# First layer of a two-layer transformer kernel: the order of TensorE's work in an attention slot, with one score chunk made a slot ahead and projections moved in front of the turned blocks

## The chip, the cores and the metric

One core of a Trainium2 chip. The metric is the device time of one execution in microseconds (us). TensorE does the matmuls, ScalarE (ACT) the exponentials and half of the copies out of PSUM, VectorE (DVE) the row maxima and the other copies, GpSimd (POOL) some elementwise work, and SyncE (SP) issues the DMAs. Each engine runs its own list of instructions in the order in which the program gives them; semaphores hold an instruction back until another engine has got far enough.

## The reference, cut to what matters

Eight batches of 512 tokens of 128 features go through two layers. The change is in the attention of the first layer, which has 16 heads of 64:

```
q = einsum('qdh,bcd->bhcq', Q, x) * sq          # x is layer-normed
k = einsum('qdh,bcd->bhcq', K, x) * sq
v = einsum('vdh,bcd->bhcv', V, x) * sv
att = einsum('bhcq,bhCq->bhcC', q, k) / d_query  # causal mask
p = softmax(att)
y = einsum('bhcC,bhCv->bhcv', p, v)
z = einsum('dvh,bhcv->bcd', W, y) * ...
```

Beside it stands a mixture of experts (32 experts and a shared one), worked as 17 units of gate, up and down products. The second layer is not touched.

## The kernel before

The first layer goes batch by batch. A batch has eight rounds, one for each pair of heads (PAIRS = 8), and then 17 expert units. A round n needs, in this order of data:

- its queries and keys: project_qk on TensorE (three products each, since every operand is split in a high and a low part), round_q and round_k on ACT (the high part), rest_q and rest_k on DVE (the low part);
- the scores in three chunks: chunk 0 is the last tile of 128 rows against 512 columns, chunk 1 is tiles 2 and 0, chunk 2 is tile 1 (CHUNKS). Each chunk fills two PSUM banks, one for each head. Score products use 64 rows of the array for each head;
- row_maxima on DVE, then exps on ACT, which write probs;
- the turned blocks: 20 transposes of 128x128 in five steps (turn_step, numbers 0, 1, 4, 3, 2 in TensorE's order), each into one bank. DVE copies steps 0, 1, 3 and 2 to the tile pt (take_turned), ACT copies step 4 (take_tile1);
- weigh_pair, the products of the turned blocks with the values, into bank 6; ACT copies the result to yt (copy_y).

PSUM has eight banks, and all of this shares them, so much of the order comes from banks: a turned step can't be written before the one that held its bank is copied, and a chunk of scores not before the bank's last reader is done. Before the change the five turned steps use banks 4 and 5 in turn, chunks 0 and 2 use banks 0 and 1, and chunk 1 banks 2 and 3.

TensorE's order is written out in slot. Slot n (n not the first of a batch) turns round n-1 and scores round n: turned steps 0 and 1 of n-1, queries n+1, chunk 0 of n, turned step 4, keys n+1, turned steps 3 and 2, chunks 1 and 2 of n, weigh_pair of n-1. The first slot of a batch (first_head) ends the batch before: two last expert units and the output projection (project_out) stand between its chunks. The function units begins with the turned steps of the last round, between the halves of the first expert unit. Each first_layer function (one in the program of ACT, one in that of DVE) holds the matching order of its engine. On DVE, route spreads the router's work over the slots.

Semaphores that matter here: pt_ready counts DVE's copies of turned steps (four in a round), pt4_ready ACT's one, y_ready ACT's copies of weighed values, qk_lo_ready the low parts, exp_done and max_ready the chunks.

Of the kernel before, what the change touches and what calls it, by code (L numbers as in the profile page):

```python
# [43 lines left out]
NCH = len(CHUNKS)  # L44
SCORE_BANK = [0, 2, 0]
SCORE_COL = {3: 0, 2: 0, 0: 384, 1: 0}
# [35 lines left out]
def build(nc, a, out_dram):  # L82
    with ExitStack() as ctx:
# [145 lines left out]
        def own_bank(n, s):  # L229


            return n >= ROUNDS0 and s == 2 and (n - ROUNDS0) % (2 * G) in range(2, 2 * G, 2)

        def turn_bank(n, s):
            return bank[6] if own_bank(n, s) else bank[TURN_BANK[s]]

# [3 lines left out]
        def rows_bank(b):  # L240

            return bank[6] if b < B - 1 else bank[7]

        UNIT_BANKS = [bank[0:2], bank[2:4]]

        def qk_banks(n):

            if n < ROUNDS0 and n % PAIRS < 2:
                return (bank[4], bank[5]) if n % PAIRS == 0 else (bank[6], bank[5])
            return bank[6], bank[7]  # L250
# [124 lines left out]

        def max_count(n, c):
            return n * NCH + ([1, 2, 3] if first_round(n) else [1, 3, 2])[c]

        def score_bank(n, c):

            return [6, 0, 6][c] if n >= ROUNDS0 and first_round(n) else SCORE_BANK[c]

# [323 lines left out]
        def _(act):  # L706
# [41 lines left out]
            def exps(rnd, c):  # L748
# [7 lines left out]
                last.then_inc(exp_done, 1)  # L756

            def take_values(b, fills):
# [51 lines left out]
            def copy_combt(b):  # L810
                act.wait_ge(combt_done, b + 1)
                act.activation(combt, bank[7][:, 0:P], ACT.Copy).then_inc(combt_ready, 1)

            def first_layer(b):
# [4 lines left out]
                for p in range(PAIRS):  # L819
                    n = b * PAIRS + p  # L820
                    if p == 0:
                        exps(n, 0)
                    if p < PAIRS - 1:
                        round_q(n + 1, SCALE0)
                    if p:
                        take_tile1(n - 1)
                        exps(n, 0)
                    if p < PAIRS - 1:
                        round_k(n + 1)
                    else:  # L830
                        copy_combt(b)
                    if p == 0:
                        exps(n, 1)
                    exps(n, 2)
                    if p == 0 and b:
                        copy_acc(b - 1)
# [5 lines left out]
                    if p:  # L842
                        copy_y(n - 1)
                        exps(n, 1)
# [5 lines left out]
                take_tile1(b * PAIRS + PAIRS - 1)  # L850
                for u in range(UNITS):
# [143 lines left out]
        def _(dve):  # L995
# [184 lines left out]
            def first_layer(b):  # L1180
                for p in range(PAIRS):
                    n = b * PAIRS + p
                    if p == 0:
                        row_maxima(n, 0)
                        row_maxima(n, 1)
                        rest_q(n + 1, SCALE0)
                        rest_k(n + 1)
                        row_maxima(n, 2)
                    else:
# [3 lines left out]
                        if p < PAIRS - 1:  # L1193
                            rest_q(n + 1, SCALE0)
                        elif b:
                            add_rows(b - 1)
                        take_turned(n - 1, [3, 2])
                        row_maxima(n, 2)
                        if p < PAIRS - 1:
                            rest_k(n + 1)  # L1200
                        row_maxima(n, 1)
                    route(b, p)
                n = b * PAIRS + PAIRS - 1
                take_turned(n, range(0, 2))
                invert_sums(n)
                for u in range(UNITS):
# [174 lines left out]
        def _(pe):  # L1381
# [78 lines left out]
            def turn_step(rnd, s):  # L1460
# [15 lines left out]
                if s == 3:  # L1476
                    pe.wait_ge(pt_ready, rnd * (TURNS - 1) + 2)
                blocks = [(s % 2, 3, j) for j in range(4)] if s < 2 else [(s % 2, 2, j) for j in range(3)] + [(s % 2, 0, 0)]
                if s == 4:
# [40 lines left out]
            def project_unit(b, u):  # L1520
                n = b * UNITS + u
                if u >= 2:
                    pe.wait_ge(su_done, n - 1)
                else:
                    pe.wait_ge(exp_done, exp_count((b + 1) * PAIRS - 1, 2 - u))
                half_unit(b, u, 0)
# [56 lines left out]
            def turn_weights(b):  # L1583

                pe.wait_ge(comb_ready, b + 1)
                nc.tensor.transpose(bank[7][:, 0:P], rexp[:, :, :].rearrange("p t e -> p (t e)"), ident[:, :]).then_inc(combt_done, 1)

            def score0(n, c):
                score_chunk(n, c, n % 2, ROWS0)

            def first_chunks(b):
                n = b * PAIRS
                pe.wait_ge(qk_lo_ready, n * 2 + 2)
                if b:
                    pe.wait_ge(su_done, b * UNITS)
                score0(n, 0)

            def slot(n, head):
# [6 lines left out]
                if p == 1:  # L1605
                    pe.wait_ge(qk_lo_ready, n * 2 + 2)
                turn_step(n - 1, 0)
                turn_step(n - 1, 1)
                if p < PAIRS - 1:
                    pe.wait_ge(y_ready, n - 1) if p > 1 else pe.wait_ge(qk_lo_ready, n * 2 + 1)  # L1610
                    project_qk(n + 1, [0])
                pe.wait_ge(qk_lo_ready, n * 2 + 2)
                pe.wait_ge(exp_done, exp_count(n - 1, 2))
                score0(n, 0)
                turn_step(n - 1, 4)
                if p == 1:
                    pe.wait_ge(acc_copied, b) if b else pe.wait_ge(logits_taken, 1)
                if p < PAIRS - 1:
                    project_qk(n + 1, [1])
                else:  # L1620
                    turn_weights(b)
                    pe.wait_ge(y_ready, n - 1)
                    if b:
                        turn_acc(b - 1)
                turn_step(n - 1, 3)
                turn_step(n - 1, 2)
                score_rest(n, n % 2, ROWS0)
                if p < PAIRS - 1:
                    pe.wait_ge(qk_lo_ready, (n + 1) * 2 + 1)
                elif b:  # L1630
                    pe.wait_ge(x1_ready, b)
                weigh_pair(n - 1)

            def first_head(b):

                if b:
                    project_out(b - 1, 0)
# [3 lines left out]
                    unit_down(b - 1, UNITS - 1)  # L1641
                first_chunks(b)
                score0(b * PAIRS, 1)
                if b:
                    project_out(b - 1, 2)
                pe.wait_ge(v_taken, (b + 1) * FILLS)
                project_qk(b * PAIRS + 1, range(2))
                pe.wait_ge(exp_done, exp_count(b * PAIRS, 0))
                score0(b * PAIRS, 2)
                if b:  # L1650
                    project_out(b - 1, 3).then_inc(acc_done, 1)

            def units(b):
                n = (b + 1) * PAIRS - 1
                turn_step(n, 0)
                turn_step(n, 1)
                pe.wait_ge(exp_done, exp_count(n, 2))
                half_unit(b, 0, 0)
                turn_step(n, 4)
                half_unit(b, 0, 1).then_inc(gu_done, 1)  # L1660
                turn_step(n, 3)
                turn_step(n, 2)
                project_unit(b, 1)
# [38 lines left out]
            for b in range(B):  # L1702
                if b == 1:
                    pe.wait_ge(act_setup, 1)
                for p in range(PAIRS):
                    slot(b * PAIRS + p, lambda: first_head(b))
                if b == 0:
# [285 lines left out]
```

## Time and profile before

| | |
|---|---|
| median of 3 runs | 1213.09 us (1210.03 to 1213.88) |
| span of the profiled execution | 1209.2 us (first to last instruction; what lies around it is not in the profile) |
| TensorE busy | 1189.8 us, 98% |
| DVE busy | 990.7 us, 82% |
| ACT busy | 819.7 us, 68% |
| GpSimd busy | 409.9 us, 34% |
| granted TensorE clock | 1.000 |

A busy TensorE in this table is one that has an instruction under way by a modelled end; gaps of a few tenths between products can be inside it. Times in the trace are counted from the start of the span. Each batch of the first layer takes about 121 us, and its attention part, from the first score product to the transpose that follows the last weigh_pair (line 1495), 75.7 us.

### The profile page before, as it was taken

The numbers are of one execution on the slowest core, as the hardware profiler recorded it, in microseconds if no ns is written. First come the engines' busy times: TensorE is split into PE (matmuls) and PEld (weight loads), VectorE is DVE, ScalarE is ACT, GpSimd is POOL, SyncE is SP. The second block draws the span as 40 slices with busy tenths as digits, with TensorE's granted clock in tenths as the row PEclk, the third lists the DMA queues.
The fourth block names the chain that finished last, engine by engine and source line by source line (L and its number), as shares of the span: only waits on it lengthen the run. The fifth ranks groups of instructions, "written<-read, shape, count | busy, mean of one in ns | idle before, by whom it ended". The sixth has DMA issues, their size and how long they took to land.

```text
span 1209.2 us, 23949 instructions
## 1 busy us (share of the span) xinstructions
PE 1189.8 (98%) x8908; PEld 887.1 (73%) x8908; DVE 990.7 (82%) x1918; ACT 819.7 (68%) x2174; POOL 409.9 (34%) x364
## 2 busy tenths in 40 slices
PE   8999999999999999999999999999999999999998
PEld 6777677767776777677767776777677767767766
DVE  6888588968886889688968896888788878988886
ACT  6785577567756775677567756775677768767875
POOL 2216420640064006400640064006400658535820
PEclk9999999999999999999999999999999999999999
DMA  7004300410041004200420042004200420000000
GB/s 258 1 30 134 97 1 21 132 61 2 20 134 62 1 19 134 62 1 19 135 62 1 20 134 62 1 17 136 62 1 16 138 62 2 7 12 19 1 11 27
DMA packets 44292, 63.93 MB, mean 53 GB/s; under 512 B 8144, under 2 KB 18384, under 8 KB 43920
## 3 DMA queue, kind: packets, MB, share of 16 engines
q1 hardware_dynamic: 44176, 62.39, 16.6%
q8 instruction: 72, 1.18, 0.4%
q14 instruction: 44, 0.36, 0.1%
HBM read 59.48 MB, written 2.88 MB: 52 GB/s over the span
## 4 chain that ended last, share of the span: by engine, by line
PE 82%; DVE 10%; ACT 4%; issue 2%; DMA 1%; SPq 1%; POOL 0%; DVEq 0%; ACTq 0%; POOLq 0%
PE psum L1435 14%; PE psum L1483 14%; PE psum L1505 12%; PE psum L64 9%; PE psum L66 9%; PE psum L65 9%; PE psum L1542 5%; DVE mneg L1123 2%; ACT probs L754 2%; PE psum L1444 2%; PE psum L1718 1%; DVE sg L1173 1%; PE psum L1509 1%; PE psum L1781 1%; DVE sg L1163 1%
## 5 line engine op out<-in xcount | busy, mean ns | idle before, releaser
L754 ACT ACTIVATE probs<-psum,mneg 128x512 f32<-128x512 f32 (+3 forms) x640 | 329.7, 529 | 127.1 <-DVE mneg L1123 122.5
L1123 DVE TENSOR_REDUCE mneg<-psum 128x2 f32<-128x1024 f32 (+2 forms) x320 | 253.6, 820 | 99.9 <-PE psum L1444 99.5
L1114 DVE COPY pt<-psum 128x512 f32<-128x512 f32 x320 | 205.2, 682 | 29.7 <-PE psum L1483 27.9
L1483 PE MATMUL psum<-ident,probs 128*128 128x128 f32 x1600 | 223.3, 278 | 6.1 <-DVE pt L1114 2.1
L1483 PEld LDWEIGHTS psum<-ident,probs 128*128 128x128 f32 x1600 | 176.5, 140 | 37.9 <-issue 19.5
L561 POOL TENSOR_TENSOR qk_lo<-sg,qk_hi 128x512 fp32r<-128x512 f32 x64 | 92.7, 1455 | 162.0 <-ACT qk_hi L798 162.0
L525 POOL TENSOR_TENSOR rstd<-var,mhalf 128x4 f32<-128x4 f32 x7 | 7.1, 1012 | 399.8 <-DVE var L1009 399.8
L1505 PE MATMUL psum<-pt,v_all 128*64 128x384 f32 (+5 forms) x1088 | 142.6, 412 | 0.0
L754 ACT ACTIVATION_READ_ACCUMULATOR probs<-psum,mneg 128x1 f32 x640 | 131.8, 206 | 0.0
L1435 PE MATMUL psum<-qk_hi 64*128 64x512 f32 (+7 forms) x640 | 121.6, 375 | 2.2 <-ACT probs L754 1.9
L1505 PEld LDWEIGHTS psum<-pt,v_all 128*64 128x64 f32 (+1 forms) x1088 | 69.5, 135 | 66.2 <-issue 50.7
L64 PE MATMUL psum<-xt_hi,gu_hi 128*128 128x512 f32 x272 | 110.7, 407 | 0.0
L66 PE MATMUL psum<-xt_hi,gu_lo 128*128 128x512 f32 x272 | 107.7, 396 | 0.0
L65 PE MATMUL psum<-xt_lo,gu_hi 128*128 128x512 f32 x272 | 107.4, 395 | 0.0
L557 POOL TENSOR_TENSOR yt<-yt,rrow 128x512 f32<-128x512 f32 x64 | 99.2, 1556 | 21.4 <-DMA rrow<-sums 21.3
L1435 PE MATMUL psum<-qk_lo,qk_hi 64*128 64x512 f32 (+7 forms) x640 | 103.5, 319 | 0.0
L1435 PE MATMUL psum<-qk_hi,qk_lo 64*128 64x512 f32 (+7 forms) x640 | 103.3, 318 | 0.0
L1173 DVE TENSOR_TENSOR sg<-sg,crow 128x512 f32<-128x512 f32 x88 | 96.4, 1096 | 6.0 <-DMA crow<-weights 3.1
L808 ACT ACTIVATE sg<-psum 128x512 f32<-128x512 f32 x96 | 57.1, 595 | 54.1 <-PE psum L66 53.9
L1435 PEld LDWEIGHTS psum<-qk_hi 64*128 64x128 f32 (+1 forms) x640 | 60.1, 184 | 42.9 <-issue 38.4
L1163 DVE TENSOR_TENSOR sg<-sg,psum 128x512 f32<-128x512 f32 x96 | 65.3, 680 | 20.1 <-ACT sg L808 20.1
L798 ACT ACTIVATE qk_hi<-sg 128x512 fp32r<-128x512 f32 x96 | 60.3, 628 | 31.3 <-DVE sg L1173 31.3
(275 smaller groups left out, 2422.4 us busy)
## 6 DMA issues: line engine op xcount, KB each, us to landing
crow<-weights SPq DMA_DIRECT2D x256, 128.0 KB, 3.0
rrow<-sums SPq DMA_DIRECT2D x128, 128.0 KB, 3.0
gu_raw<-in_gu SPq DMA_DIRECT2D x1, 2176.0 KB, 11.5
x_all<-in_x SPq DMA_DIRECT2D x8, 256.0 KB, 6.4
out_rows<-x_all SPq DMA_DIRECT2D x7, 256.0 KB, 2.3
down_raw<-in_down SPq DMA_DIRECT2D x1, 1088.0 KB, 13.7
wqkv_raw<-in_wqkv SPq DMA_DIRECT2D x1, 896.0 KB, 6.8
wqkv_raw<-in_wqkv SPq DMA_DIRECT2D x1, 512.0 KB, 5.0
```

What stands on the lines that cost most here:

```text
L64: nc.tensor.matmul(out, lh, rh, start=start, stop=False, **kw)
L65: nc.tensor.matmul(out, lh, rl, start=False, stop=False, **kw)
L66: return nc.tensor.matmul(out, ll, rh, start=False, stop=stop, **kw)
L557: pool.tensor_tensor(yt[:, p, :], yt[:, p, :], rrow[:, n % RROWS, :], ALU.mult).then_inc(y_divided, 1)
L561: pool.tensor_tensor(hm_lo[u % 3], sg[u % 3], hm_hi[u % 3].bitcast(F32), ALU.subtract).then_inc(pool_lo_ready, 1)
L754: last = act.activation(probs[:, h * HALF + PROB[t]:h * HALF + PROB[t] + w], bank[score_bank(rnd, c) + h][:, o:o + w], ACT.Exp, bias=mneg[ ...
L1114: dve.tensor_copy(turned_rows(rnd)[:, s % 2, :, 3 - s // 2, :], turn_bank(rnd, s).rearrange("p (j q) -> p j q", q=P)).then_inc(pt_ready, 1)
L1123: last = dve.tensor_reduce(mneg_h[:, :, t], psum[:, b:b + 2, o:o + P * (t + 1)], AX, ALU.max, negate=True)
L1173: dve.tensor_tensor(sg[u % 3], sg[u % 3], crow[:, m % CROWS, :], ALU.mult).then_inc(hm_ready, 1)
L1435: mm(bank[score_bank(rnd, c) + h][:, o:o + w], ql[r, 0, qs_], kl[r, 1, ks], start=i == 0 and n == 0, stop=False, **K)
L1483: last = nc.tensor.transpose(turn_bank(rnd, s)[:, i * P:(i + 1) * P], probs[:, v:v + P], ident[:, :])
L1505: last = mm(Y[c:c + m, first * P:T], v(k), rows_t[:, k, first:TILES, :].rearrange("p t q -> p (t q)"), start=(k == 0), stop=(k == TILES - ...
```

## The change

Three things are moved, and banks follow.

1. Slot n now does round n as a whole, but for its chunk 0: chunks 1 and 2 of n, chunk 0 of n+1 (score_group), then weigh_pair of n-1, queries and keys of n+2, and last all five turned steps of n. ACT makes the exponentials of chunk 0 of n+1 at the end of slot n (next_exps), after it has rounded the queries and keys of n+2.
2. Chunk 2's scores move to banks 4 and 5, and the five turned steps get a bank each: 2, 3, 7, 5, 4 (TURN_BANK0, for steps 0 to 4). Queries go to bank 7, keys to bank 6, except for the first two pairs of a batch. Steps are guarded by other waits than before (turn_step0).
3. The first slot of a batch projects round 1 directly behind its chunk 0 and rounds it on ACT before the exponentials of chunk 1; the projection of round 2 now waits in that slot for the copy of the batch before's output sum (acc_copied).

No operation is added or taken away. The core of the diff:

```diff
-SCORE_BANK = [0, 2, 0]
+SCORE_BANK = [0, 2, 4]
+        TURN_BANK0 = [2, 3, 7, 5, 4]
...
 # ACT, first_layer
                     if p == 0:
                         exps(n, 0)
+                        round_q(n + 1, SCALE0)
+                        round_k(n + 1)
+                    exps(n, 1)
+                    if p:
+                        copy_y(n - 1)
+                        exps(n, 2)
+                    else:
+                        exps(n, 2)
+                        if b:
+                            copy_acc(b - 1)
+                    if p < PAIRS - 2:
+                        round_q(n + 2, SCALE0)
+                        round_k(n + 2)
+                    if p == PAIRS - 2:
+                        copy_combt(b)
                     if p < PAIRS - 1:
-                        round_q(n + 1, SCALE0)
-                    if p:
-                        take_tile1(n - 1)
-                        exps(n, 0)
...
+                        next_exps(n + 1, 0)
+                        next_exps(n + 1, 1)
+                    take_tile1(n)
...
 # DVE, first_layer
-                        take_turned(n - 1, range(0, 2))
-                        row_maxima(n, 0)
-                        invert_sums(n - 1)
...
+                    row_maxima(n, 1)
+                    row_maxima(n, 2)
+                    if p < PAIRS - 1:
+                        row_maxima(n + 1, 0)
                     route(b, p)
+                    if p < PAIRS - 2:
+                        rest_q(n + 2, SCALE0)
+                    take_turned(n, [0])
+                    if p < PAIRS - 2:
+                        rest_k(n + 2)
+                    elif p == PAIRS - 1 and b:
+                        add_rows(b - 1)
+                    take_turned(n, [1])
+                    invert_sums(n)
+                    if p < PAIRS - 1:
+                        take_turned(n, [3, 2])
...
 # TensorE
+            def turn_step0(n, s):
+
+                b, p = n // PAIRS, n % PAIRS
+                pe.wait_ge(exp_done, exp_count(n, [1, 1, 2, 2, 2][s]))
+                if s == 2 and p < PAIRS - 2:
+                    pe.wait_ge(qk_lo_ready, (n + 2) * 2 + 1)
+                if s == 2 and p == PAIRS - 2:
+                    pe.wait_ge(combt_ready, b + 1)
+                turn_blocks(n, s)
+
+            def score_group(n):
+
+                b, p = n // PAIRS, n % PAIRS
+                if p:
+                    pe.wait_ge(pt_ready, (n - 1) * (TURNS - 1) + 2)
+                score0(n, 1)
+                if p:
+                    pe.wait_ge(pt4_ready, n)
+                    pe.wait_ge(pt_ready, (n - 1) * (TURNS - 1) + 3)
+                if p < PAIRS - 1:
+                    pe.wait_ge(qk_lo_ready, (n + 1) * 2 + 2)
+                score0(n, 2)
+                if p < PAIRS - 1:
+                    pe.wait_ge(exp_done, exp_count(n, 0))
+                    score0(n + 1, 0)
+
+            def slot(n):
...
                 if p == 0:
-                    head()
-                    return
...
+                    first_head(b)
+                score_group(n)
+                if p:
+                    weigh_pair(n - 1)
+                elif b:
+                    project_out(b - 1, 3).then_inc(acc_done, 1)
+                if p < PAIRS - 2:
+                    if p:
+                        project_qk(n + 2, [0])
+                        pe.wait_ge(y_ready, n)
+                        project_qk(n + 2, [1])
+                    else:
+                        pe.wait_ge(acc_copied, b) if b else pe.wait_ge(logits_taken, 1)
+                        project_qk(n + 2, range(2))
+                elif p == PAIRS - 2:
+                    turn_weights(b)
+                elif b:
+                    pe.wait_ge(y_ready, n)
+                    turn_acc(b - 1)
+                turn_step0(n, 0)
+                turn_step0(n, 1)
                 if p < PAIRS - 1:
...
+                    turn_step0(n, 4)
+                    turn_step0(n, 3)
+                    turn_step0(n, 2)
```

## Rows read from the trace of the kernel before

**Rows 1.** The page: span, parts 1 and 2.
```profile
span 1209.2 us, 23949 instructions
...
PE 1189.8 (98%) x8908; PEld 887.1 (73%) x8908; DVE 990.7 (82%) x1918; ACT 819.7 (68%) x2174; POOL 409.9 (34%) x364
...
PEclk9999999999999999999999999999999999999999
```

**Rows 2.** Waits of the whole span: engine, line, releaser: us in total, times, longest.
```profile
PE psum L1483 <- DVE pt L1114: 2.1, 5, 0.6
```

**Rows 3.** Windows: busy by engine (instructions), clock, DMA share, GB/s.
```profile
382.74:458.41 75.67, 75.67 (x676) 54.97 (x675) 61.42 (x122) 53.85 (x163) 2.02 (x2) 1.00 0.04 13
...
407.92:416.68 8.76, 8.76 (x84) 6.45 (x82) 7.30 (x17) 6.46 (x20) 0.00 (x0) 1.00 0.01 3
...
450.95:458.41 7.46, 7.46 (x54) 5.50 (x52) 5.07 (x9) 5.90 (x14) 2.02 (x2) 1.00 0.35 105
17.85:93.40 75.55, 72.91 (x664) 53.13 (x663) 62.84 (x121) 60.28 (x173) 18.18 (x14) 1.00 0.16 42
```

**Rows 4.** Timeline of TensorE in one slot: start, us, engine, line.
```profile
407.92 1.09 PE L1483 MATMUL psum<-ident,probs 128*128 128x128 f32 x8
...
409.63 0.18 PEld L1435 LDWEIGHTS psum<-qk_hi 64*128 64x128 f32 x2 [0.36 <-issue]
409.64 0.50 PE L1435 MATMUL psum<-qk_hi 64*128 64x512 f32 x2
...
410.62 0.66 PE L1483 MATMUL psum<-ident,probs 128*128 128x128 f32 x4
...
412.77 0.45 PE L1435 MATMUL psum<-qk_hi 64*128 64x384 f32 x2
...
414.37 2.16 PE L1505 MATMUL psum<-pt,v_all 128*64 128x384 f32 x16
```

**Rows 5.** Timeline of ACT in the same slot and the next one's start.
```profile
408.53 0.58 ACT L754 ACTIVATE probs<-psum,mneg 128x384 f32<-128x384 f32 x1
...
410.33 0.62 ACT L767 ACTIVATE qk_hi<-psum 128x512 fp32r<-128x512 f32 x1
...
411.99 0.69 ACT L754 ACTIVATE probs<-psum,mneg 128x512 f32<-128x512 f32 x1
...
415.10 0.47 ACT L754 ACTIVATE probs<-psum,mneg 128x256 f32<-128x256 f32 x1 [1.18 <-DVE mneg L1123]
...
415.93 0.20 ACT L754 ACTIVATION_READ_ACCUMULATOR probs<-psum,mneg 128x1 f32 x1
...
416.80 0.60 ACT L788 ACTIVATE yt<-psum 128x512 f32<-128x512 f32 x1 [0.67 <-PE psum L1509]
417.29 0.57 ACT L754 ACTIVATE probs<-psum,mneg 128x384 f32<-128x384 f32 x1
```

**Rows 6.** Timeline of DVE in the same slot.
```profile
410.73 1.23 DVE L1123 TENSOR_REDUCE mneg<-psum 128x2 f32<-128x1024 f32 x1 [0.76 <-PE psum L1444]
...
411.98 0.64 DVE L1103 SCALAR_TENSOR_TENSOR qk_lo<-psum,qk_hi 128x512 fp32r<-128x512 f32 x1
412.54 1.28 DVE L1114 COPY pt<-psum 128x512 f32<-128x512 f32 x2
...
414.99 0.68 DVE L1108 TENSOR_TENSOR qk_lo<-psum,qk_hi 128x512 fp32r<-128x512 f32 x1
...
415.58 1.28 DVE L1123 TENSOR_REDUCE mneg<-psum 128x2 f32<-128x768 f32 x2
```

**Rows 7.** Timeline of the first slot of the fourth batch.
```profile
387.44 0.60 ACT L767 ACTIVATE qk_hi<-psum 128x512 fp32r<-128x512 f32 x1 [0.91 <-PE psum L66]
...
388.06 0.69 DVE L1103 SCALAR_TENSOR_TENSOR qk_lo<-psum,qk_hi 128x512 fp32r<-128x512 f32 x1 [1.82 <-ACT qk_hi L767]
...
388.64 1.98 PE L1542 MATMUL psum<-yt,w_out 128*128 128x512 f32 x4
```

**Rows 8.** Timeline of ACT in the first batch: a weight split at a slot's end.
```profile
25.17 1.33 ACT L730 ACTIVATE gu_hi<-gu_raw 128x1280 fp32r<-128x1280 f32 x1
```

More of the change, by code:

```diff
@@ L232, in own_bank @@
             return n >= ROUNDS0 and s == 2 and (n - ROUNDS0) % (2 * G) in range(2, 2 * G, 2)
+        TURN_BANK0 = [2, 3, 7, 5, 4]
+        TURN_BANK0_FIRST = [2, 3, 7, 5, 4]
         def turn_bank(n, s):
+            if n < ROUNDS0:
+                return bank[(TURN_BANK0 if n % PAIRS else TURN_BANK0_FIRST)[s]]
             return bank[6] if own_bank(n, s) else bank[TURN_BANK[s]]
@@ L242, in rows_bank @@
             return bank[6] if b < B - 1 else bank[7]
+        WEIGHTS_BANK = bank[7]
         UNIT_BANKS = [bank[0:2], bank[2:4]]
         def qk_banks(n):
-            if n < ROUNDS0 and n % PAIRS < 2:
-                return (bank[4], bank[5]) if n % PAIRS == 0 else (bank[6], bank[5])
+            if n < ROUNDS0:
+                return (bank[4], bank[5]) if n % PAIRS == 0 else (bank[6], bank[5]) if n % PAIRS == 1 else (bank[7], bank[6])
             return bank[6], bank[7]
@@ L376, in max_count @@
         def max_count(n, c):
+            if n < ROUNDS0:
+                return n * NCH + c + 1
             return n * NCH + ([1, 2, 3] if first_round(n) else [1, 3, 2])[c]
         def score_bank(n, c):
-            return [6, 0, 6][c] if n >= ROUNDS0 and first_round(n) else SCORE_BANK[c]
+            if n < ROUNDS0:
+                return SCORE_BANK[c]
+            return [6, 0, 6][c] if first_round(n) else SCORE_BANK1[c]
         exp_count = max_count
@@ L756, in exps, with next_exps @@
                 last.then_inc(exp_done, 1)
+            def next_exps(rnd, h):
+                act.wait_ge(max_ready, max_count(rnd, 0))
+                act.wait_ge(turned, turn_count(rnd - 1, h))
+                t = CHUNKS[0][0]
+                o, s = h * HALF + PROB[t], slice(h * TILES + t, h * TILES + t + 1)
+                last = act.activation(probs[:, o:o + T], bank[score_bank(rnd, 0) + h], ACT.Exp, bias=mneg[:, s], accum_out=rsum[:, rnd % 2, s])
+                if h:
+                    last.then_inc(exp_done, 1)
             def take_values(b, fills):
@@ L811, in copy_combt @@
                 act.wait_ge(combt_done, b + 1)
-                act.activation(combt, bank[7][:, 0:P], ACT.Copy).then_inc(combt_ready, 1)
+                act.activation(combt, WEIGHTS_BANK[:, 0:P], ACT.Copy).then_inc(combt_ready, 1)
             def first_layer(b):
@@ L1585, in turn_weights @@
                 pe.wait_ge(comb_ready, b + 1)
-                nc.tensor.transpose(bank[7][:, 0:P], rexp[:, :, :].rearrange("p t e -> p (t e)"), ident[:, :]).then_inc(combt_done, 1)
+                nc.tensor.transpose(WEIGHTS_BANK[:, 0:P], rexp[:, :, :].rearrange("p t e -> p (t e)"), ident[:, :]).then_inc(combt_done, 1)
             def score0(n, c):
                 score_chunk(n, c, n % 2, ROWS0)
[L1591 to L1598, printed above, removed]
+            def turn_step0(n, s):
[21 more added lines that the diff above has]
+            def slot(n):
                 p = n % PAIRS
@@ L1602, in slot @@
                 if p == 0:
-                    head()
-                    return
[L1605 to L1608, printed above, removed]
-                if p < PAIRS - 1:
[L1610 to L1632, printed above, removed]
+                    first_head(b)
[19 more added lines that the diff above has]
+                turn_step0(n, 1)
+                if p < PAIRS - 1:
+                    turn_step0(n, 4)
+                    turn_step0(n, 3)
+                    turn_step0(n, 2)
             def first_head(b):
+                n = b * PAIRS
                 if b:
@@ L1641, in first_head @@
                     unit_down(b - 1, UNITS - 1)
-                first_chunks(b)
-                score0(b * PAIRS, 1)
+                pe.wait_ge(qk_lo_ready, n * 2 + 2)
+                if b:
+                    pe.wait_ge(su_done, b * UNITS)
+                score0(n, 0)
+                pe.wait_ge(v_taken, (b + 1) * FILLS)
+                project_qk(n + 1, range(2))
                 if b:
                     project_out(b - 1, 2)
[L1646 to L1651, printed above, removed]
             def units(b):
                 n = (b + 1) * PAIRS - 1
-                turn_step(n, 0)
-                turn_step(n, 1)
-                pe.wait_ge(exp_done, exp_count(n, 2))
                 half_unit(b, 0, 0)
-                turn_step(n, 4)
+                turn_step0(n, 4)
                 half_unit(b, 0, 1).then_inc(gu_done, 1)
-                turn_step(n, 3)
-                turn_step(n, 2)
+                turn_step0(n, 3)
+                turn_step0(n, 2)
+                pe.wait_ge(pt_ready, n * (TURNS - 1) + 2)
+                if b:
+                    pe.wait_ge(x1_ready, b)
                 project_unit(b, 1)
@@ L1705, in _ @@
                 for p in range(PAIRS):
-                    slot(b * PAIRS + p, lambda: first_head(b))
+                    slot(b * PAIRS + p)
                 if b == 0:
```

32 lines of the change are left out of this document (3 added, 29 removed).

## The prediction, made before the changed kernel was run

> **What bounds the kernel now.** I read the page first: TensorE is busy 98% of the span at full clock, the others have room [rows 1]. Busy ends are modelled, so I asked the waits whether it really never stands: in the whole span its longest entry of waiting for a copy of turned blocks is 2.1 us in 5 waits [rows 2]. Then the windows. The attention part of a batch takes 75.67 us without idle time on TensorE (75.6 to 75.7 in every batch but the first, which has 75.55 with 2.6 idle); inside it a plain slot takes 8.76 us, five times in a batch, while DVE works 7.30 to 7.8 and ACT 6.46 of it [rows 3]. So time is won only by making TensorE's own list shorter, and lost wherever the new order makes it stand. The rest of the work (31.87 of 75.67) lies in the first slot, the last two and the head of the units.
>
> **What the change takes away.** No operation goes. What goes is switching between score products (64 rows) and 128-row work: before a slot enters the scores twice, now once. The gap in front of such an entry is 0.36 in which weights waited for nothing shown, and chunk 0 with its masks takes 409.64 to 410.62 = 0.98, of which three product pairs at the 0.24 that follow one another and the masks' 0.08 explain 0.8 [rows 4]. One visit fewer is thus worth between 0 (masks now stand between score products, and the change from weighing to projecting is new and not in the trace) and 0.34; I take 0.17. TensorE alone would need 8.6 us for a slot. The Trainium skill (TensorE: Matmul & The Clock Gate, Step-by-step: what each phase is for) says that weight loads are pulled ahead of running matmuls where row groups don't conflict or a background buffer is free; read as always, that would leave no gap and so no gain, slots of 8.76. The 0.36 shows that a gap is there.
>
> **What the change makes wait: the plain slot (p = 1 to 5).** Before, five pieces lay between one round's steps, and everyone was served while TensorE did something else. Now all scores stand together, all turned steps stand together, and chunk 1 of slot n+1 may start only when DVE has copied steps 0 and 1 of n (banks 2 and 3). On DVE those copies stand behind rest_q(n+2), on ACT round_q(n+2) stands behind the exponentials of chunk 2, and those behind copy_y(n-1), which waits for this slot's weigh_pair. That is a ring. From the first product of chunk 1:
>
> - chunks 1 and 2 with their masks, 412.77 to 414.37: 1.60. Chunk 0 of n+1 inside the scores: 0.98 less the 0.10 of entering, 0.88. First weighing product to the start of copy_y, 414.37 to 416.80: 2.43. Together 4.91 [rows 4, 5]. ACT is free by then: the maxima of chunk 1 start some 1.2 in and take 1.28, the exponentials 408.53 to 410.33 = 1.80, so 4.33 [rows 5, 6].
> - ACT: copy_y to the next start 0.49; chunk 2's two exponentials 415.10 to about 416.03, 0.93; round_q 0.62 to its end [rows 5]; handing over 0.02 to 0.03 [rows 7]. 6.98 so far.
> - DVE: rest_q 0.56 to the next start; copy of step 0 0.60; rest_k 0.59; copy of step 1 0.68 to its end [rows 6]; 0.05 to TensorE. **9.46.**
>
> Can a step come later than its place in the ring? Step 0 is turned in time: keys are projected from 5.56 (y_ready), and keys with four transposes take less than the 1.72 of eight transposes and three products (407.92 to 409.64), 7.3 against the 7.54 at which DVE comes [rows 4]. round_k ends at 7.4, before 8.14. DVE's route (1.2 at most in a slot) lies in the 2.5 us for which it now waits in front of rest_q: nothing. ACT's chunk 0 (1.34, 411.99 to 413.33) and take_tile1 run from 7.5 to 9.2 and chunk 2 of the next slot wants them at 10.4: nothing [rows 5]. DVE ends steps 3 and 2 at 10.7, when the next maxima become due: nothing, but no room left. So TensorE, done at 8.6, stands some 0.85 in front of chunk 1, and a slot takes 9.46 for 8.76: +0.70, +3.5 for five.
>
> **The first slot (b > 0).** From chunk 0: maxima end at 2.33, exponentials at 3.70, round_q and round_k at 4.80, rest_k at 5.6. Chunk 1 stands behind the projections (1.4) and project_out (1.98 [rows 7]), starts at 4.5 and is scored at 5.75; maxima till 7.03, exponentials of chunks 1 and 2 (1.80 + 0.93) till 9.79, copy_acc till 10.39. TensorE has been done with project_out since 9.1 and stands: the projection of round 2 wants that bank. It starts at 10.44; round_q can start 0.97 later and takes 0.62, then the four DVE steps 2.43: chunk 1 of slot 1 at 14.5.
>
> **The last slots.** Slot 6 has no projections, so step 4 comes up at about 5.7, and chunk 2's exponentials end at 4.91 + 0.49 + 1.03 = 6.43; 12 transposes at 0.11 and the entry: 7.95. Slot 7 has no chunk 0: weighed at 4.03, ACT busy until 4.33, copy_y until 4.93, and turn_acc waits for it though TensorE was free at 3.9. Then 0.44 for turn_acc and the 7.46 that steps 0 and 1, the units' head and weigh_pair take unchanged [rows 3]: 12.9.
>
> **Sum.** 14.5 + 5 x 9.46 + 7.95 + 12.9 = 82.65 for 75.67: +7.0 a batch. In the first batch no project_out and no copy_acc: slot 0 12.7, the last 11.9, in all 79.9 for 75.55, +4.3; ACT's weight splits (1.33 [rows 8]) now follow take_tile1 and end at 10.6, before the next exponentials are due at 12. 7 x 7.0 + 4.3 = 53. Units and second layer keep their lists: 0. The span goes from 1209.2 to 1262; the median lies 3.9 above the span, so 1213.1 + 53 = **1266 us**.
>
> **The rivals.**
> - *The ring is hidden, the kernel gets faster.* TensorE then pays only its own list, 0.17 to 0.34 less in each of about 7 slots and 8 batches: 1194 to 1203. It needs a ring under 8.6. Even if weighed values came for free, ACT's other path (4.33 + 0.49 in place of 4.91 + 0.49) gives 8.88. So two copies or an order of waits would have to be other than I read them: 5%.
> - *The ring closes near the old slot, no change.* Decides at 8.7: three quarters of a us must be missing, partly by ACT or DVE being quicker when TensorE stands. With the first slot's wait still there: 1209 to 1220. 6%.
> - *DVE is the bound.* It has no room between step 2's copy and the next maxima. The ring would be DVE's: all its work at full durations, with every start after the end before. Then rest_q, copy and rest_k cost 0.64 + 0.68 + 0.68, not 1.75, slots take 9.7 and, as steps 3 and 2 come late as well, up to 10: 10 to 22 us more, 1276 to 1288. Against it: two copies took 1.28, not 2 x 0.68 [rows 6]. 9%. The Trainium skill (VectorE: DVE Perf Modes, The DRAIN you can't avoid) states just this, that the next op does not start until the pipe is empty; these rows disagree for ops that wait for nothing.
> - *Partly hidden.* First and last slots wait as worked out but plain slots take 9.0 to 9.2 (copies earlier than I place them): 1245 to 1256. 10%.
> - The forecast, 9.3 to 9.6 a plain slot and within 0.7 of my sum for the others: 1254 to 1278. 70%.
>
> **Range and chances.** 0.3% is about what a measurement of this kernel can tell from no change. 1247 to 1283 holds the forecast, most of the partly hidden case and half of DVE's: 8 in 10. Faster 0.05, within 0.3% 0.04, slower 0.91 (the no-change case reaches beyond 0.3% by a third).
>
> **What the trace after would show.** Plain slots of 9.46 from one first product of line 1435's 384-column form to the next; in front of each, TensorE idle for about 0.85 and released by DVE's copy (line of take_turned); ACT idle in front of copy_y by about 0.5; DVE idle for 1.5 to 2.5 in front of rest_q, released by round_q; in first slots about 1.3 released by copy_acc; in slots 7 about 1.0 released by copy_y. TensorE's busy share falls from 98% to about 94%, its clock stays. I am wrong if TensorE's idle time in front of chunk 1 is small, or if it is released by something else than the copy of step 1.

## The result, and the profile after

The changed kernel takes 1267.97 us (median of 4 runs, 1267.71 to 1269.03) for 1212.49 us of the kernel before (4 runs): 1.046 times as long, 95% interval 1.0443 to 1.0474. The forecast was 1266 with a range of 1247 to 1283. So the time grew by 55.5 us; the spans of the two profiled executions differ by 56.7, since the profiled one of the kernel before was about 1.5 us shorter than its median.

The page of the changed kernel: span, busy time, TensorE's busy tenths and clock in 40 slices, and the chain that ended last.

```profile
span 1265.9 us, 23805 instructions
...
PE 1190.5 (94%) x8908; PEld 894.5 (71%) x8908; DVE 978.4 (77%) x1918; ACT 810.0 (64%) x2174; POOL 406.3 (32%) x364
...
PE   8999999999999999999998999899989999999998
...
PEclk9999999999999999999999999999999999999999
...
PE 59%; DVE 20%; ACT 15%; issue 3%; DMA 1%; SPq 1%; POOL 0%; DVEq 0%; ACTq 0%; POOLq 0%
```

TensorE's matmuls (8908) and its busy time (1190.5 for 1189.8 [rows 1]) are the same; the span has grown by 56.7. So the time is idle time of TensorE, and the chain that ended last now runs through DVE and ACT for a third of the span; in the kernel before they had a seventh of it:

```profile
PE 82%; DVE 10%; ACT 4%; issue 2%; DMA 1%; SPq 1%; POOL 0%; DVEq 0%; ACTq 0%; POOLq 0%
```

The waits of TensorE in the whole span (line of the waiting work, releaser, us in total, times, longest) say where:

```profile
PE psum L1456 <- DVE pt L1137: 35.9, 48, 0.8
PE psum L65 <- ACT rrow L824: 7.8, 7, 1.1
PE psum L1571 <- ACT yt L810: 7.4, 7, 1.1
PE psum L1508 <- ACT probs L766: 5.5, 12, 0.7
PE psum L1456 <- DVE qk_lo L1131: 3.2, 8, 1.9
```

The first line is new: 48 times, in front of chunk 1 in slots 1 to 6 of each of the eight batches, the score products of line 1456 wait for DVE's copy of turned blocks, 35.9 us in all (before slot 1 the wait is 0.3, before the others 0.8). The second is the projection of round 2 waiting for copy_acc, the third turn_acc waiting for copy_y. The fourth is for the most part turned step 4 of slot 6 waiting for chunk 2's exponentials (0.5 in slot 6 of the fourth batch), the fifth the first slot's wait for rest_k, 1.9 in the first batch and 0.2 in the others. Together about 60 us.

Windows of the fourth batch, as in [rows 3]: the attention part, its first slot, a plain slot, slot 6; then the attention part of the first batch and three us of it. The columns are as in those rows; the number behind the five engines is the granted clock.

```profile
402.76:485.66 82.90, 75.58 (x676) 55.61 (x676) 60.82 (x122) 52.40 (x163) 2.02 (x2) 1.00 0.03 12
402.76:417.17 14.41, 12.79 (x87) 8.47 (x87) 7.99 (x13) 8.79 (x26) 0.00 (x0) 1.00 0.01 2
426.72:436.26 9.54, 8.70 (x83) 6.56 (x84) 7.21 (x18) 6.25 (x20) 0.00 (x0) 1.00 0.01 2
464.80:472.72 7.92, 7.44 (x78) 5.63 (x78) 6.73 (x15) 4.96 (x19) 0.00 (x0) 1.00 0.04 11
18.95:99.30 80.35, 72.93 (x664) 54.77 (x664) 60.26 (x122) 59.89 (x174) 17.88 (x14) 0.98 0.13 35
25.00:28.00 3.00, 3.00 (x22) 2.11 (x21) 2.12 (x4) 2.22 (x10) 0.00 (x0) 0.50 0.21 53
```

The part takes 82.90 for 75.67, +7.2; a plain slot 9.54 for 8.76, of which TensorE is busy 8.70. (Four of the five plain slots of a batch take 9.53 to 9.55, the fifth 9.46.) And the ring itself, one plain slot in the timeline:

```profile
426.72 0.45 PE L1456 MATMUL psum<-qk_hi 64*128 64x384 f32 x2 [0.84 <-DVE pt L1137]
...
427.73 0.37 PE L1456 MATMUL psum<-qk_hi 64*128 64x256 f32 x2
...
429.19 2.16 PE L1530 MATMUL psum<-pt,v_all 128*64 128x384 f32 x16
...
431.62 0.60 ACT L810 ACTIVATE yt<-psum 128x512 f32<-128x512 f32 x1 [0.39 <-PE psum L1534]
...
432.11 0.47 ACT L766 ACTIVATE probs<-psum,mneg 128x256 f32<-128x256 f32 x1
...
433.01 0.61 ACT L789 ACTIVATE qk_hi<-psum 128x512 fp32r<-128x512 f32 x1
...
433.07 2.35 PE L1508 MATMUL psum<-ident,probs 128*128 128x128 f32 x20
...
433.72 0.69 DVE L1126 SCALAR_TENSOR_TENSOR qk_lo<-psum,qk_hi 128x512 fp32r<-128x512 f32 x1 [2.22 <-ACT qk_hi L789]
434.33 0.68 DVE L1137 COPY pt<-psum 128x512 f32<-128x512 f32 x1
...
434.93 0.68 DVE L1131 TENSOR_TENSOR qk_lo<-psum,qk_hi 128x512 fp32r<-128x512 f32 x1
...
435.52 0.68 DVE L1137 COPY pt<-psum 128x512 f32<-128x512 f32 x1
...
436.26 0.45 PE L1456 MATMUL psum<-qk_hi 64*128 64x384 f32 x2 [0.84 <-DVE pt L1137]
```

Read it as a relay. Chunk 1 starts at 426.72; weigh_pair at 429.19; copy_y, which waited for it, at 431.62 (4.90 in); then on ACT chunk 2's exponentials and round_q (433.01); DVE had waited 2.22 for that one; then rest_q, step 0, rest_k, step 1, whose end at 436.20 lets chunk 1 of the next slot go, 9.54 after the first. TensorE stood for 0.84.

### The profile page after: what moved, and what is told of

Its sections match the earlier page's. It is cut to its first block, busy times and chain, and to the rows that moved or that the text cites. A ratio compares the mean times of both kernels' runs of the same rounds, so it can differ in the third digit from the quotient of the medians.

```text
span 1265.9 us, 23805 instructions
## 1 busy us (share of the span) xinstructions
PE 1190.5 (94%) x8908; PEld 894.5 (71%) x8908; DVE 978.4 (77%) x1918; ACT 810.0 (64%) x2174; POOL 406.3 (32%) x364
## 4 chain that ended last, share of the span: by engine, by line
PE 59%; DVE 20%; ACT 15%; issue 3%; DMA 1%; SPq 1%; POOL 0%; DVEq 0%; ACTq 0%; POOLq 0%
PE psum L1456 12%; PE psum L1530 10%; ACT probs L766 9%; PE psum L65 7%; PE psum L67 7%; PE psum L66 7%; DVE pt L1137 5%; DVE mneg L1146 4%; DVE qk_lo L1126 3%; PE psum L1508 3%; DVE qk_lo L1131 3%; ACT yt L810 3%; ACT qk_hi L789 2%; PE psum L1565 2%; PE psum L1465 2%
## 5 line engine op out<-in xcount | busy, mean ns | idle before, releaser
L766 ACT ACTIVATE probs<-psum,mneg 128x256 f32<-128x256 f32 (+3 forms) x528 | 254.3, 494 | 217.6 <-DVE mneg L1146 216.6
L1146 DVE TENSOR_REDUCE mneg<-psum 128x2 f32<-128x1024 f32 (+2 forms) x320 | 244.6, 819 | 45.9 <-PE psum L1465 43.9
L1508 PE MATMUL psum<-ident,probs 128*128 128x128 f32 x1600 | 199.8, 274 | 8.2 <-ACT probs L766 5.5
L1456 PE MATMUL psum<-qk_hi 64*128 64x512 f32 (+7 forms) x640 | 121.7, 376 | 40.9 <-DVE pt L1137 35.9
L1126 DVE SCALAR_TENSOR_TENSOR qk_lo<-psum,qk_hi 128x512 fp32r<-128x512 f32 x72 | 49.5, 688 | 119.2 <-ACT qk_hi L789 119.1
L1456 PEld LDWEIGHTS psum<-qk_hi 64*128 64x128 f32 (+1 forms) x640 | 60.6, 185 | 70.3 <-DVE pt L1137 47.3
L766 ACT ACTIVATION_READ_ACCUMULATOR probs<-psum,mneg 128x1 f32 x528 | 108.2, 205 | 0.0
```

The source lines that it names most:

```text
L766: last = act.activation(probs[:, h * HALF + PROB[t]:h * HALF + PROB[t] + w], bank[score_bank(rnd, c) + h][:, o:o + w], ACT.Exp, bias=mneg[ ...
L1146: last = dve.tensor_reduce(mneg_h[:, :, t], psum[:, b:b + 2, o:o + P * (t + 1)], AX, ALU.max, negate=True)
L1456: mm(bank[score_bank(rnd, c) + h][:, o:o + w], ql[r, 0, qs_], kl[r, 1, ks], start=i == 0 and n == 0, stop=False, **K)
L1508: last = nc.tensor.transpose(turn_bank(rnd, s)[:, i * P:(i + 1) * P], probs[:, v:v + P], ident[:, :])
```

## Experiments

Each kernel is the changed one with a short edit. Ratios are to the kernel before the change, from runs on the same chip.

**Is it the place in DVE's order, or DVE's amount of work?** Two edits: one moves work and adds none, the other adds work and moves none. The first moves the copy of step 1 ahead of rest_k:

```diff
-                    take_turned(n, [0])
+                    take_turned(n, [0, 1])
                     if p < PAIRS - 2:
                         rest_k(n + 2)
...
-                    take_turned(n, [1])
                     invert_sums(n)
```

> The changed kernel, but on DVE the copy of turned step 1 stands in front of rest_k, directly behind the copy of step 0. Same work, same amount. Theory (ring): rest_k, 0.60 to the next start, leaves the ring and nothing takes its place, since TensorE's own list is 8.70: plain slots go from 9.54 to 8.94, the first slot gains 0.2. About 3.2 us a batch, 25 in all: 1243. Rival (DVE's total work is the bound): the order on DVE changes nothing, 1268. Rival (the ring closes over chunk 2, which wants rest_k): plain slots stay within 0.1 of 9.54, 1264 to 1268.

Measured: 1255.5 us, ratio 1.036 (1.0343 to 1.0374); a plain slot 9.27, not 8.94. Moving work that stays the same in amount gains 12 us, so the order matters, but that is only half of the 25 that the ring gave. What was late next is in the timeline: chunk 2's first product (256 columns) comes 1.32 after chunk 1's, where in the changed kernel it was 1.01 (427.73 after 426.72).

```profile
430.14 0.44 PE L1455 MATMUL psum<-qk_hi 64*128 64x384 f32 x2 [0.24 <-DVE pt L1137]
...
430.72 1.24 DVE L1137 COPY pt<-psum 128x512 f32<-128x512 f32 x2
...
431.46 0.39 PE L1455 MATMUL psum<-qk_hi 64*128 64x256 f32 x2
```

The copies of steps 3 and 2 start at 430.72; the first of them ends at about 431.4, and chunk 2, which wants the bank of step 3, starts at 431.46. That copy had slipped behind rest_k; rest_k itself, ahead of it on DVE, can't have been the last thing awaited. Slot 6 became longer for the same reason, 8.24 for 7.92, while the first slot gained 0.4 (14.00 for 14.41).

The second edit adds work to DVE and moves nothing, one more reduction of 1.2 us a slot:

```diff
                     if p < PAIRS - 1:
+                        if p:
+                            bk = score_bank(n + 1, 0)
+                            dve.wait_ge(scored, max_count(n + 1, 0))
+                            dve.tensor_reduce(table_two, psum[:, bk:bk + 2, :], AX, ALU.max, negate=True)
                         row_maxima(n + 1, 0)
```

> The changed kernel with one more row maximum over two banks (1024 columns, 1.2 us) on DVE in each slot but the first and the last of a batch, in front of the maxima of chunk 0 of the next round; its result is used by nobody. It falls into the 2.2 us for which DVE waits in front of rest_q. Theory (ring): in most slots nothing, since 2.97 + 1.28 + 0.6 + 1.2 + 1.2 + route ends before round_q at 6.97; up to 0.3 where route is long: 1268 to 1275. Rival (DVE's total work is the bound): 1.2 us in each of 48 slots, 1326.

Measured: 1265.8 us, ratio 1.045 (1.0432 to 1.0467), the same as the changed kernel's 1.046 (1.0443 to 1.0474). The window of a plain slot is 9.54 with DVE at work for 8.55 of it:

```profile
435.07:444.61 9.54, 8.69 (x84) 6.55 (x84) 8.55 (x22) 6.24 (x20) 0.00 (x0) 1.00 0.01 3
```

DVE's total is not the bound: its work may grow by more than 1 us a slot for nothing, if it lands in the wait in front of rest_q.

**Both gates of DVE's order taken away.** Step 3 is copied before rest_k too, and TensorE waits for the low part of the keys where it needs them:

```diff
-                if p < PAIRS - 1:
+                if p == 0:
                     pe.wait_ge(qk_lo_ready, (n + 1) * 2 + 2)
                 score0(n, 2)
                 if p < PAIRS - 1:
+                    pe.wait_ge(qk_lo_ready, (n + 1) * 2 + 2)
...
 # DVE
-                    take_turned(n, [0])
+                    take_turned(n, [0, 1])
...
+                    take_turned(n, [3])
+                    invert_sums(n)
                     if p < PAIRS - 2:
                         rest_k(n + 2)
...
-                        take_turned(n, [3, 2])
+                        take_turned(n, [2])
```

> As the run with step 1 in front of rest_k, and besides DVE copies step 3 before rest_k too, and TensorE waits for the low part of the keys only behind chunk 2, where chunk 0 of the next round needs it. In the earlier run a plain slot took 9.26 and not 8.94, because chunk 2 waited 0.3 for the copy of step 3 (bank 5), which had slipped behind rest_k. Theory (ring, with that second gate taken away): plain slots 8.95, 0.3 x 5 x 8 = 12 us less than 1255: about 1243. Rival (the missing 0.3 is something else, as scores slowed by a neighbouring bank): slots stay at 9.26, 1255.

Measured: 1238.7 us, ratio 1.021 (1.0197 to 1.0228); a plain slot is 8.93, as the ring says. The 0.3 that was missing was step 3's bank. The total came out 4 us lower than I expected. I had counted 0.3 in plain slots alone; three of the five gained 0.33, and slot 6 came back from 8.24 to 7.91. That makes 1.8 a batch and 14.2 in all, and the two spans differ by 14.5 (1253.2 and 1238.7). The first slot stayed at 14.00. The medians, from different series, differ by 16.9, and the 2.4 between the two figures stay open.

```profile
425.18:434.11 8.93, 8.69 (x82) 6.54 (x83) 7.32 (x20) 6.16 (x21) 0.00 (x0) 1.00 0.01 2
```

**Is the wait for the weighed values part of the ring?** ACT does copy_y behind chunk 2's exponentials:

```diff
                     if p:
-                        copy_y(n - 1)
                         exps(n, 2)
+                        copy_y(n - 1)
```

> The changed kernel, but on ACT copy_y(n-1) stands behind the exponentials of chunk 2, not in front of them. Theory (the ring: weigh_pair, copy_y, exponentials of chunk 2, round_q, rest_q, copies of steps 0 and 1, chunk 1 of the next slot): the wait for weigh_pair leaves the ring, ACT's own list takes its place: 4.38 + 0.90 + 0.49, then the 3.25 from round_q on, so a plain slot goes from 9.54 to about 9.0. Slot 6 gains about 0.65 (step 4 waits less), slot 7 loses about 0.9 (turn_acc waits for a later copy_y). About 2.6 us a batch, 21 in all: 1247, still slower than before the change. Rival (DVE's work as a whole is the bound, or TensorE's own list): plain slots stay at 9.5, and with slot 7 later the time is the same or up to 7 us more: 1268 to 1275.

Measured: 1267.1 us, ratio 1.046 (1.0443 to 1.0479). My 1247 was wrong, and the rival's 1268 to 1275 comes close, but not for its reason: a plain slot went from 9.54 to 9.34, so the wait is in the ring. A batch without a fall of the clock gained 0.7 and not 2.6: plain slots gave 0.9, slot 6 the 0.7 that I expected (7.22 for 7.92), and the last slot took 0.9 back. Two things ate the rest. In the plain slot:

```profile
431.75 0.62 ACT L810 ACTIVATE yt<-psum 128x512 f32<-128x512 f32 x1
...
432.42 0.50 PE L65 MATMUL psum<-xt_hi,wqkv_hi 128*128 128x512 f32 x1 [0.21 <-ACT yt L810]
...
433.86 0.69 DVE L1137 COPY pt<-psum 128x512 f32<-128x512 f32 x1 [0.21 <-PE psum L1508]
```

A later copy_y makes the keys late (they take its bank), the turned steps stand behind the keys on TensorE, and now DVE waits for step 0, 0.21, where it used to come too late for it. I had added up ACT's own path (4.38 + 0.90 + 0.49 + 3.25 = 9.02), but not the path that changes engine in between. And in the last slot of a batch the wait of turn_acc grew from 1.05 to 1.97, after which TensorE's granted clock fell to 1.2 GHz for a while in two of the seven batches. It fell a third time in the expert units of the first batch, after a wait of 0.79. Windows: a plain slot, the attention parts of the third batch (no fall) and the fourth, the time after that wait, and the third fall:

```profile
435.80:445.14 9.34, 8.90 (x83) 6.54 (x84) 7.51 (x21) 6.26 (x21) 0.00 (x0) 1.00 0.01 2
...
275.19:357.37 82.18, 76.38 (x676) 55.56 (x676) 61.17 (x122) 52.34 (x163) 2.02 (x2) 1.00 0.04 12
402.71:486.46 83.75, 77.94 (x677) 56.94 (x676) 61.09 (x122) 52.33 (x163) 2.02 (x2) 0.98 0.04 11
...
475.00:480.00 5.00, 3.03 (x18) 2.63 (x17) 1.89 (x4) 1.93 (x9) 0.73 (x1) 0.80 0.42 143
480.00:485.00 5.00, 5.00 (x28) 3.86 (x28) 2.11 (x5) 3.22 (x5) 0.00 (x0) 0.86 0.00 0
...
123.00:126.40 3.40, 3.40 (x10) 2.62 (x9) 1.52 (x2) 1.59 (x5) 1.64 (x2) 0.51 0.58 165
```

83.75 less 82.18, 1.6 us, is what one fall cost here. The third cost as much: from the first attention part to the second 48.93 us pass, and 47.32 in the changed kernel. Without its three falls this run would have been some 5 us shorter, as an estimate from these differences.

**Are the first and the last slot's waits additive?** ACT copies the output sum ahead of chunk 2's exponentials; TensorE turns steps 0 and 1 ahead of turn_acc, and DVE copies step 1 ahead of add_rows.

```diff
 # ACT
                     else:
-                        exps(n, 2)
                         if b:
                             copy_acc(b - 1)
+                        exps(n, 2)
...
 # TensorE
-                elif b:
-                    pe.wait_ge(y_ready, n)
-                    turn_acc(b - 1)
                 turn_step0(n, 0)
                 turn_step0(n, 1)
+                if p == PAIRS - 1 and b:
+                    pe.wait_ge(y_ready, n)
+                    turn_acc(b - 1)
```

> The changed kernel with only the batch's first and last slot mended: in the first, ACT copies the output sum (copy_acc) before the exponentials of chunk 2; in the last, TensorE turns steps 0 and 1 before turn_acc, and DVE copies step 1 before add_rows. Theory: 0.7 of the first slot and 0.6 of the last are these two waits, 1.3 us in seven batches, 9 in all: 1259; plain slots stay at 9.54. Rival (these waits only shift to the next place): 1266 to 1268.

Measured: 1261.5 us, ratio 1.041 (1.0391 to 1.0422), 6.5 less than the changed kernel, where I had expected 9; a plain slot stays at 9.53. Both waits were real and their removal stays gained, though the first slot gives 0.4 and not 0.7, and the last 0.5 and not 0.6. The projection of round 2 still waits up to 0.7 for copy_acc, and copy_acc itself 0.4 for the output projection.

**What is left if no ring closes?** The plain slot reordered on all three engines, the operations and banks unchanged. The edit reaches the ends of a batch too: in the first slot the projection of round 2 stands behind steps 0 and 1, in the last slot steps 0 and 1 stand ahead of turn_acc, and step 1 is copied ahead of add_rows.

```diff
 # TensorE, in place of queries, keys, steps 0, 1, 4, 3, 2
...
+                elif 0 < p < PAIRS - 2:
+                    project_qk(n + 2, [0])
                 turn_step0(n, 0)
                 turn_step0(n, 1)
+                if p == 0:
+                    pe.wait_ge(acc_copied, b) if b else pe.wait_ge(logits_taken, 1)
+                    project_qk(n + 2, range(2))
+                elif p < PAIRS - 2:
+                    pe.wait_ge(y_ready, n)
+                    project_qk(n + 2, [1])
+                elif p == PAIRS - 1 and b:
+                    pe.wait_ge(y_ready, n)
+                    turn_acc(b - 1)
...
 # ACT
                     elif p:
                         exps(n, 2)
                         copy_y(n - 1)
...
                         round_q(n + 2, SCALE0)
...
                         next_exps(n + 1, 0)
                         next_exps(n + 1, 1)
...
                         round_k(n + 2)
                     take_tile1(n)
...
 # DVE
                     take_turned(n, [0])
...
                         rest_q(n + 2, SCALE0)
                     take_turned(n, [1])
...
                         take_turned(n, [3])
...
                         rest_k(n + 2)
...
                         take_turned(n, [2])
```

> The changed kernel with its plain slot reordered so that the ring no longer closes: ACT does the exponentials of chunk 2, then copy_y, round_q, next_exps, round_k; DVE the copy of step 0, rest_q, step 1, step 3, rest_k, step 2; TensorE queries, steps 0 and 1, keys, steps 4, 3 and 2, and in the last slot steps 0 and 1 before turn_acc. Theory: every ring is now under TensorE's own list, plain slots 8.6 to 8.7, first slot 13.4, slot 6 7.3, slot 7 to the end of the part 12.3: 76.4 a batch, 1218. Rival (merging the scores costs TensorE as much as it saves, and the waits go elsewhere): plain slots 8.76 or more, 1222 and up.

Measured: 1213.6 us (11 runs), ratio 1.001 (1.0002 to 1.0019), a plain slot 8.56. With the same operations, the order alone brings back some 54 of the 55.5 us. The attention part takes 75.73 for 82.90: the five plain slots give 4.8 of that, the first slot 1.2, slot 6 0.7, the last 0.5. I had expected 76.4 a batch and 1218; plain slots and the first slot (13.25 for 13.4) came out shorter. The profiled execution also has the clock at its low level for some 10 us of the first batch, which the kernel before has not:

```profile
24.00:28.00 4.00, 3.17 (x23) 2.40 (x21) 2.65 (x5) 2.84 (x12) 0.00 (x0) 0.50 0.49 119
28.00:32.00 4.00, 4.00 (x19) 3.40 (x19) 1.92 (x5) 2.05 (x6) 0.00 (x0) 0.65 0.00 0
...
119.60:122.90 3.30, 3.30 (x10) 2.53 (x9) 1.60 (x2) 1.41 (x4) 1.53 (x2) 0.50 0.68 183
```

And with the first slot scoring chunk 1 directly behind chunk 0 again, and the first half unit ahead of the last round's steps 0 and 1 (DVE's order in the first slot follows):

```diff
                 score0(n, 0)
+                score0(n, 1)
                 pe.wait_ge(v_taken, (b + 1) * FILLS)
...
+                if p == PAIRS - 1:
...
+                    half_unit(b, 0, 0)
                 turn_step0(n, 0)
```

> The one before, and in the batch's first slot chunk 1 again directly behind chunk 0 and DVE's maxima in that order, and in the last slot the first half unit in front of turned steps 0 and 1. Theory: first slot 12.8, last slot to the end 12.0: 75.4 a batch, 0.25 less than the kernel before the change: 1210 to 1212, which is within 0.3% of it. Rival: 1216 to 1220, as the copy of the output sum is still waited for.

Measured: 1201.7 us, ratio 0.9915 (0.9903 to 0.9928): 0.85% faster than the kernel before the change. Windows of the last kernel: the fourth batch's attention part and a plain slot; then TensorE in that slot.

```profile
377.75:452.45 74.70, 74.42 (x676) 55.78 (x675) 61.10 (x122) 51.65 (x163) 2.01 (x2) 1.00 0.04 13
407.70:416.26 8.56, 8.56 (x83) 6.58 (x83) 7.40 (x20) 6.13 (x21) 0.00 (x0) 1.00 0.01 2
```

```profile
407.70 0.44 PE L1466 MATMUL psum<-qk_hi 64*128 64x384 f32 x2
...
410.17 2.16 PE L1540 MATMUL psum<-pt,v_all 128*64 128x384 f32 x16
...
412.48 0.51 PE L65 MATMUL psum<-xt_hi,wqkv_hi 128*128 128x512 f32 x1
...
413.29 1.03 PE L1518 MATMUL psum<-ident,probs 128*128 128x128 f32 x8
...
414.86 1.47 PE L1518 MATMUL psum<-ident,probs 128*128 128x128 f32 x12
416.26 0.44 PE L1466 MATMUL psum<-qk_hi 64*128 64x384 f32 x2
```

Here TensorE has no wait in a plain slot, so this is its own list, 8.56 for 8.76. Taken piece by piece, the three chunks of scores with their masks take 2.47 (407.70 to 410.17), where the kernel before spent 0.98 + 1.60 = 2.58 on them, and the queries 0.81 (412.48 to 413.29) for 0.87 (408.77 to 409.64) before, when a score product stood behind them. That is 0.17 for merging the scores. The last 0.03 is the balance of the other pieces, which stand in another order here. The changed kernel shows the same 2.47 (426.72 to 429.19), but there the gain lay under 0.84 of waiting.

I expected 1210 to 1212. The attention part took 74.7 for the 75.4 that I had added up, and the first batch's part 72.9 for 75.55 before; what made that one shorter stays open in part. Between the kernel before and this one the clock plays no part: in both profiled executions it stays at the upper level through all attention parts, and the spans differ by 9.4 (1209.2 and 1199.8). Of the 12.0 between this span and the one of the run before it, 7.1 lie in the attention parts of seven batches; the other 4.9 lie nearly all in the first batch (76.5 for 72.9 in its attention part, 48.9 for 47.3 from there to the next one), where the clock fell in that run and not in this, so they can't be put down to the edit alone.

## Why the prediction was right, by its steps

- *Nothing is removed, TensorE's list is the bound before.* Right: the busy time is the same to 0.7 us, and what was added are waits of TensorE.
- *Switches removed, 0.17 a slot between 0 and 0.34.* The pieces of the last kernel give 0.17 for it, and its whole slot is 0.20 shorter. TensorE's 8.70 of busy time in the changed kernel's slot is a little more than its list: it holds the modelled end of the last transpose. In the last kernel the next score product starts 0.07 before that end (414.86 + 1.47 against 416.26), so the changed kernel's own list is, as an estimate, 8.63, which is the 8.6 that I took.
- *The ring, 9.46.* 9.54 measured. The first leg, 4.91, measured 4.90; ACT's leg from copy_y to round_q 1.39 for 1.42; round_q to rest_q 0.71 for 0.65, rest_q 0.61 for 0.56, the last copy and its handing over 0.74 for 0.73. That it is a ring and not just a sum is shown by three edits of it (step 1 first, both copies first, copy_y later): each shortened the slot, until another gate held.
- *The last slots and the first.* Slot 6 took 7.92 for 7.95, the first slot 14.41 for 14.5, slot 7 to the end 12.94 for 12.9; in all 82.9 for 82.65. The 0.25 is the balance of plain slots that were 0.3 longer in sum and a first slot that was 0.1 shorter. The first batch took 80.35 for 79.9, for the same reason: 0.3 in the plain slots, 0.1 each in the first and the last. I had left out a fall of the clock there (0.50 in the window at 25 to 28), but it cost hardly anything. Windows of that first slot in the changed kernel and in the run with the later copy_y, where the clock did not fall:

```profile
18.95:31.77 12.82, 10.60 (x79) 8.11 (x79) 8.15 (x13) 9.11 (x29) 0.00 (x0) 0.87 0.61 145
...
18.75:31.48 12.73, 9.51 (x79) 6.91 (x79) 7.98 (x13) 9.12 (x28) 0.00 (x0) 1.00 0.64 150
```

  TensorE's work took 1.1 longer and the slot 0.1: in front of the next chunk 1 it waited 0.3 and not 1.1.
- *Sum.* I had 53. 7 x 7.2 + 4.8 = 55 in the attention parts; the span grew by 56.7. Of the rest, 1.1 lies before the first score product (18.95 for 17.84), in the start of the kernel that the change does not touch; it is of the size by which starts differ between the kernels here (17.6 to 19.3). The range held because the chain was right, not by errors that happened to cancel: no slot was off by more than about 0.1.
- *Everything costed at nothing* (route, take_tile1, ACT's weight splits, units and second layer): right. The parts between attention parts take 45.05 to 45.67 after and 45.05 to 45.46 before, the first, 47.3, and the end behind the last attention part, 266.9 for 267.0, are the same.
- *Rivals.* DVE's work as the bound is refuted by the added reduction. I had set beside that rival a rule of the Trainium skill (VectorE: DVE Perf Modes, The DRAIN you can't avoid), that the next op does not start until the pipe is empty. That was half of what the section says: it adds that a next op that is not held starts earlier, and the rows agree with this. Step 1's copy ended 0.68 after its start, but rest_q, the copy of step 0 and rest_k gave way to the next after 0.61, 0.60 and 0.59. The other rule of the Trainium skill that I weighed (TensorE: Matmul & The Clock Gate, Step-by-step: what each phase is for), read as saying that weight loads are always pulled ahead, would make merging worth nothing; the 0.17 says that entering the scores has a price here. The faster kernel that I gave 5% for this change did come about, but only with other orders on all three engines.
- *What the trace after would show.* TensorE's idle time in front of chunk 1 is 0.84 for 0.85, released by DVE's copy; DVE idles 2.22 in front of rest_q (1.5 to 2.5), ACT 0.39 in front of copy_y (0.5), turn_acc waits 1.05 (1.0), and the projection of round 2 waits 1.1 for copy_acc (1.3).
- *The clock stays.* Nearly: 0.999 on average.

## What to carry to other kernels

When an engine's list is closed up so that it switches less, ask for each piece that moved which in-order chain through the other engines it was covering, and add that chain up once round, from a start of a stage to the same start one stage later: if the sum exceeds the bound engine's list, the difference is paid in every stage. Then try to break the ring by order alone: put first on each engine what the bound engine waits for, and keep the bound engine's own pieces between a result and its use. After each such edit look again at which gate holds; a path that changes engine twice is easily missed.

## What I had not expected of the hardware

TensorE's granted clock fell from 2.4 to 1.2 GHz after single waits between dense work, but the length of the wait alone does not tell when. Behind the kernel's start, the nine traces here show three such places:

- The 1.97 wait of turn_acc (run with the later copy_y): a fall in two of seven batches.
- The wait of 1.9 for rest_k in the first slot of the first batch: a fall in the changed kernel (0.50 from 25 to 28) and in five of the edited ones, but none in the run with the later copy_y, and none after 2.0 at that place in the last kernel.
- A wait of 0.7 to 0.8 in the first batch's expert units, with twelve products on 32 rows behind it: a fall in three kernels (later copy_y, both copies first, plain slot reordered), none in the other six.

In the changed kernel's fourteen waits of up to 1.1 (copy_acc and turn_acc) and 48 of up to 0.8 it did not fall. What a fall cost depended on the place: 1.6 us where TensorE's own list was the limit, 0.1 in a first slot in which TensorE had to wait for DVE at the end anyway. The Trainium skill (TensorE: Matmul & The Clock Gate, What's actually happening) describes an activity gate with these two levels, whose watch is free-running and not reset when a kernel starts. That the effect of a wait then depends on where it lands is my reading of it; falls in some batches and not in others agree with it, and no run here tests it.
